# A scan and feed-forward layer on one core: three output tiles of each batch made in two halves

## What is computed

```
zxbcdt = u @ in_proj_w.T                       # 512 -> 2368 columns: z, x, B, C, dt
xBC = silu(causal_conv4(xBC) + conv_b)         # four taps in time, per channel
y = chunked_scan(x, dt, A, B, C) + x * D       # chunks of 64 tokens, 64 heads of 16
yg = y * silu(z)                               # 1024 channels
yn = yg * rsqrt(mean(yg * yg) + eps) * norm_weight
x = layernorm(u + yn @ out_proj_w.T)           # 1024 -> 512 columns: the output tiles
x = layernorm(x + ffn(x))                      # second stage, not touched
```

## Time and profile before

| | us |
|---|---|
| median of 3 runs | 1950.24 |
| lowest and highest | 1948.11, 1953.44 |
| profiled execution | 1956.19 |
| its span, first to last instruction | 1954.3 |
| TensorE matmuls busy | 1720.0 (88%) |
| VectorE busy | 1419.7 (73%) |
| GpSimd busy | 1002.5 (51%) |
| ScalarE busy | 938.2 (48%) |
| mean granted TensorE clock | 0.912 |

### The profile page before, as it was taken

How to read it: one execution, slowest core, us unless ns; L and a number is a source line. 1 busy time by engine, 2 the same in 40 slices (tenths; PEclk the granted TensorE clock), 3 DMA queues, 4 the chain that set the end, 5 groups by cost and what they waited for, 6 DMA issues and landing times.

```text
span 1954.3 us, 37182 instructions
## 1 busy us (share of the span) xinstructions
PE 1720.0 (88%) x11168; PEld 886.9 (45%) x11168; DVE 1419.7 (73%) x2295; ACT 938.2 (48%) x1647; POOL 1002.5 (51%) x1031
## 2 busy tenths in 40 slices
PE   2688889798888888988888897988799999999998
PEld 1244445445444454554454454455344444444443
DVE  6758757858766876686776688597677777777775
ACT  2463253344335426343533533442576666666662
POOL 0045436525444543552554365276577676777774
PEclk9898998898898888888889888987899999999999
DMA  6110140122014013112301401363011111011111
GB/s 208 48 47 26 41 98 19 39 61 73 24 41 110 26 35 79 39 38 49 90 25 41 98 26 41 70 186 54 33 33 55 33 55 45 33 54 54 33 34 54
DMA packets 214679, 109.66 MB, mean 56 GB/s; under 512 B 133796, under 2 KB 185696, under 8 KB 214496
## 3 DMA queue, kind: packets, MB, share of 16 engines
q1 hardware_dynamic: 214496, 107.37, 20.7%
HBM read 80.57 MB, written 26.76 MB: 55 GB/s over the span
## 4 chain that ended last, share of the span: by engine, by line
PE 56%; DVE 25%; issue 9%; SPq 4%; DMA 2%; ACT 2%; DVEq 1%; POOL 0%; ACTq 0%; POOLq 0%
PE ps_in L794 12%; PE ps_in L926 7%; PE ps_in L772 7%; PE ps_yo L941 6%; PE ps_yd L941 6%; PE ps_yo L852 5%; DVE pre L1271 5%; PE ps_s L926 4%; PE ps_t L926 4%; DVE mix L1360 4%; DVE state L1375 2%; PE ps_t L819 1%; SPq L543 1%; DVE res L1428 1%; PE ps_d L830 1%
## 5 line engine op out<-in xcount | busy, mean ns | idle before, releaser
L1077 ACT ACTIVATE decay<-ps_d 128x512 f32<-128x512 f32 x256 | 151.8, 593 | 333.2 <-PE ps_d L830 267.8
L772 PE MATMUL ps_in<-u_hi,w_hi 128*128 128x512 f16 (+1 forms) x608 | 238.0, 391 | 55.7 <-DVE u_lo L1258 34.1
L1360 DVE TENSOR_TENSOR mix<-decay,gb 128x512 f32<-128x512 f32 x256 | 227.1, 892 | 63.0 <-PE ps_yd L842 30.3
L1660 POOL TENSOR_TENSOR xend<-xpad,decay 128x256 f32<-128x256 f32 x256 | 180.7, 726 | 160.0 <-PE ps_yo L865 132.4
L794 PE MATMUL ps_in<-w_out,zg 128*128 128x512 f32 x512 | 253.0, 651 | 6.1 <-DVE pre L1271 6.1
L772 PE MATMUL ps_in<-u_lo,w_hi 128*128 128x512 f16 (+1 forms) x608 | 237.4, 390 | 0.0
L772 PE MATMUL ps_in<-u_hi,w_lo 128*128 128x512 f16 (+1 forms) x608 | 236.7, 389 | 0.0
L1752 POOL TENSOR_TENSOR gate_sum<-gate_sum,gate_part 128x512 f32<-128x512 f32 x88 | 142.2, 1616 | 104.6 <-DVE gate_part L1581 104.2
L1271 DVE SCALAR_TENSOR_TENSOR pre<-ps_in,cws,pre 128x511 f32<-128x511 f32 (+2 forms) x240 | 178.9, 746 | 8.6 <-ACT pre L1016 2.8
L794 PEld LDWEIGHTS ps_in<-w_out,zg 128*128 128x128 f32 x512 | 107.6, 217 | 133.3 <-issue 124.5
L852 PE MATMUL ps_yo<-bc,state 128*128 128x64 f32 x896 | 152.2, 341 | 16.9 <-DVE state L1375 16.8
(11 more groups left out here) (182 smaller groups left out, 3844.3 us busy)
## 6 DMA issues: line engine op xcount, KB each, us to landing
ebc<-e_dram SPq DMA_DIRECT2D x256, 64.0 KB, 2.6
u<-u_t SPq DMA_DIRECT2D x9, 1024.0 KB, 5.2
res<-u_tok SPq DMA_DIRECT2D x32, 256.0 KB, 2.7
x_dram<-res SPq DMA_DIRECT2D x32, 256.0 KB, 2.0
xa<-x_dram SPq DMA_DIRECT2D x8, 1024.0 KB, 5.7
xr<-x_dram SPq DMA_DIRECT2D x32, 256.0 KB, 2.6
out<-xr SPq DMA_DIRECT2D x32, 256.0 KB, 2.0
fw_words<-gu_words SPq DMA_DIRECT2D x32, 176.0 KB, 3.0
```

The source lines that it names most:

```text
L772: last = mm(ps_in[bk][0:m, :], w[:, k, col:col + m], u[:, k, :], start=(k == 0 and j == 0), stop=(k == KT - 1 and j == 2))
L1077: ac(decay[:, n % NG, :, :].rearrange("p a b -> p (a b)"), ps_d[n % 2][:, :], ACT.Exp).then_inc(e_done, 1)
L1360: v.tensor_tensor(mix[:, n % NG, :, :], decay[:, n % NG, :, :], gb[:, c % 2, 0:CH].unsqueeze(1).broadcast_to([P, CT, CH]), ALU.mult).then_ ...
L1660: g_.tensor_tensor(xend[:, pairs, :], xpad[:, c % 2, pairs, :], decay[:, g, :, CH - 1:CH].broadcast_to([P, CT, 2 * HD]), ALU.mult).then_in ...
```

## The change

`out_proj` takes a range of its eight matmuls. The waits stand ahead of the first, the release behind the last. `use_in` on TensorE makes matmuls 4 to 7 of an output tile in the tile's own slot, and matmuls 0 to 3 in the slot before, behind that slot's own uses. For o0, o1 and o2 these are slots 13, 21 and 29. o3, in the tail, goes through `use` and stays whole. No other engine's list changes.

```diff
-            def out_proj(st, tt):
+            def out_proj(st, tt, tiles=range(CT)):
                 bk, free, _ = st.bank(f"o{tt}")
-                pe.wait_ge(gate_done, st.scan * NC + 2 * tt + 2)
-                need(pe, in_free[bk], free)
-                for k in range(CT):
+                if 0 in tiles:
+                    pe.wait_ge(gate_done, st.scan * NC + 2 * tt + 2)
+                    need(pe, in_free[bk], free)
+                for k in tiles:
                     last = mm(ps_in[bk][:, :], zg[:, k, tt * P:(tt + 1) * P], w_out[:, k, :],
                               start=(k == 0), stop=(k == CT - 1))
-                last.then_inc(in_full[bk], 1)
+                if CT - 1 in tiles:
+                    last.then_inc(in_full[bk], 1)
...
             def use_in(st, slot):
                 for name in st.at(slot):
-                    use(st, name)
+                    if name[0] == "o":
+                        out_proj(st, int(name[1]), range(CT // 2, CT))
+                    else:
+                        use(st, name)
+                for name in st.at(slot + 1) if slot + 1 < SLOTS else []:
+                    if name[0] == "o":
+                        out_proj(st, int(name[1]), range(CT // 2))
```

## The result

The changed kernel takes 1987.01 us (median of 4 runs, 1978.71 to 1990.10); the kernel before, on the same chips, 1949.66 us. The ratio is 1.0182, 95% interval 1.0147 to 1.0217: slower by 1.5 to 2.2%, some 37 us. The forecast was 1979.3 us, +29.1.

A forecast was written before the change was run, and what follows sets the result against it. TensorE alone was taken to set the end from `within` to `res`. Seven batches at +34.2 us in all, less 5.1 in the last, gave +29.1; against the median 1950.24 us that is 1979.3, range 1955 to 2004.

The forecast's parts named there:

- The wait for the taps: TensorE's first half waits for VectorE's taps, ending 3.9 us after `within` starts today; total wait about 134 us plus fourth tiles.
- The state's wait: TensorE's 0.62 us wait for the state, ahead of `from_before`, goes because the state is then long ready.
- The full-clock sum: From the old start of `within` to `res` at full clock: 14.24 us for first and second tile, 13.58 for the third.
- The clock comes back 4.0 us after the first pass: TensorE starts the first half at 1.2 GHz after its pause and stays there 4.0 us, losing 2.0 us a tile.
- 3.3 us of new wait: Each split tile pays 3.3 us of new wait on TensorE; the shorter low-clock stretch gives 2 of them back.
- Low stretches about as many, and shorter: In the profile after, TensorE's stretches at 1.2 GHz would be about as many as before, and shorter.
- Per tile +1.48, +1.33, +2.08: Added time from `within` to `res` for first, second, third tile: +4.9 a batch, +34.2 us over seven batches.
- The last batch gains 5.1 us: No projection, so no taps in the way: first tile unchanged, second gains 2.9 us, third 2.2, together -5.1.
- the clock at once: Rival: in the split tiles the clock comes back as soon as today, loss 1.15 us; +11.3 us, 1961.5; chance 0.15.
- the clock low throughout: Rival: the clock stays low through the whole first half, loss 3.44 us a tile; 2014 us; chance 0.08.
- Rival 4: Nothing measurable: VectorE's 4.5 to 6.7 us of waiting for the tile takes up the shift; 1951 us; chance 0.11.
- Rival 3: First half fills the pause ahead of `within` if taps end below some 2.4 us after its old start; 1801; chance 0.04.

The follow-up runs named there:

- the pause filled: The changed kernel with 28 extra matmuls ahead of the wait for the taps in slots 13, 21 and 29, first seven batches: 1947.35 us, ratio 0.9960.
- the fastest one: The changed kernel with VectorE's taps of x0, x3, x6 one slot earlier and 8 extra matmuls ahead of the first half: 1865.54 us, ratio 0.9544.

## Why the prediction was right

Point by point, as the prediction put it:

- *The wait for the taps comes to the surface, 3.9 us after the old start of `within`.* Right in all 21 tiles. The first pass comes 4.17 us after `y_all` at o0, 4.09 at o1 and 4.17 at o2, less 0.14 for `within`'s own start: 4.0 us, and 3.93 were taken. That is 0.07 to 0.15 us after the taps end, as named. The wait for the taps grew from 6.1 to 147.5 us, where 134 plus that of the fourth tiles was named; the third tiles, whose pause was longer before, wait 7.7 us and not 6.4. Moving the half behind `within` (ratio 1.0011) and moving the taps ahead of it (0.9725) both remove the loss, the one cause from two sides.
- *The state's wait goes, and the other engines are covered.* Right: `mixing` and `y_before` start late, by 3.07 and 1.36 us of idle time, and VectorE still waits 2.25 us for the tile.
- *The full-clock sum, 14.24 us from the old start of `within`, 14.38 from `y_all`.* With the pause filled, o0 takes 14.63: the sum is 0.25 us short, of which 0.1 is in the first pass. For o2 13.72 was the sum on that scale, and it took 14.01.
- *The clock comes back 4.0 us after the first pass, a loss of 2.0.* It came back 4.33, 3.83 and 4.12 us after it (between 2.8 and 6.1 in single tiles), 4.1 in the mean. The rows after a pause came nearer than those of the output tiles, which said 2.3. That the mean of four rows met the mean of 21 tiles to 0.1 us is in part luck: single tiles spread by 3 us, and o2 split alone had it back after 3.2 us, o1 split alone after 4.9. The run with the pause filled puts the loss at 1.9 in the mean.
- *3.3 us of new wait, and the shorter low stretch gives 2 of them back.* Right in kind, too large in both: 2.6 to 3.0 us of wait, and 1.0, 1.6 and 0.2 us back by the table above. The two errors have opposite signs, and their difference came out nearly right.
- *Low stretches about as many, and shorter.* Not so in the tiles: they have 9.8, 10.7 and 10.2 us where they had 10.2, 10.2 and 7.8. What is less is the work that falls into them.
- *Per tile +1.48, +1.33, +2.08; 34.2 us for 21.* The tiles gave +1.87, +1.40, +2.41, or 39.7, so this term was 5.5 us too small, mainly by the full-clock sum of o0 and o2 (0.25 and 0.29 us). It stood at 34.75 at the last batch because of things the prediction did not have: in the seven heads of batches the clock was at the low level for 90.6 us before and for 67.1 after, and they are 7.4 us shorter; and the last batch's o0, for which no change was expected, is 1.7 us longer, with waits of 0.40 us for GpSimd and 0.59 for a DMA ahead of its first half. So the size of the total is in part luck, while its sign and the term itself are not.
- *The last batch gains 5.1 us.* It gained 5.2, but divided otherwise: o1 and o2 gained 2.6 (14.36 to 11.78, from the start of `within` before and of the first pass after) and 0.9 (13.02 to 12.08), not 2.9 and 2.2. The `res` of o3 follows that of o2 1.5 us sooner (13.34 us against 14.86), where a low stretch of 3.4 us is gone.
- *Total +29.1.* The profiled executions say +29.7. The medians say +37, interval 29 to 42 us; the changed kernel's four runs spread over 11 us, and the profiled one is the second fastest.

Of the rivals, the clock at once (1961.5) and the clock low throughout (2014) both lie outside the four runs. Rival 4, that nothing can be measured, is excluded by the interval. Rival 3 named its point of decision, where the taps end; the run that moved the taps has shown that it decides.

## What to carry to other kernels

Work that is moved ahead in an in-order list takes its waits with it, and everything it is moved past then waits for them: look up, for each moved step, when its latest wait is met, not whether there is idle time in front. If the wait is late, move what ends it first; the same split that lost 1.8% won 2.7% once the taps stood a slot earlier. And price a pause of TensorE with the clock that follows it: a few cheap matmuls in pauses of 2.4 to 3.7 us were worth 2.3% here, though they compute nothing.

## What was not expected of the hardware

The clock also falls around a short pause, and it can fall when the dense work has already begun. With the taps early, TensorE stood 1.90 us, and the granted clock of the stretch with the pause and of the next one is

```profile
305.00:307.40 2.40, 0.58 (x4) 0.30 (x3) 2.33 (x5) 1.21 (x3) 0.59 (x1) 1.00 0.00 0
307.40:311.30 3.90, 3.82 (x5) 1.65 (x6) 3.76 (x8) 0.00 (x0) 1.58 (x1) 0.57 0.00 0
```

full during the pause and low for most of the first half behind it. This order is the rare one: in two of the 21 tiles the clock fell after the first pass, in the other 19 up to 2.7 us ahead of it, which at o1 is ahead of the pause itself. The pause does not stand alone, either: TensorE had stood 1.25 us ahead of the small matmuls in front of it,

```profile
304.48 0.38 PE L786 MATMUL ps_in<-ones,ssum 128*128 128x1 f32 x2 [1.25 <-DVE pre L1279]
```

and from there to the pause it was at work for 1.1 us (304.48 to 305.58). In these tiles the clock came back 4.6 to 5.9 us after the first pass in the mean of each of the three tiles, later than after the pause of 6.4 us in the changed kernel (4.1): a shorter pause did not bring a shorter low stretch into the dense work.

The five operations of `dt_second` on VectorE (`dtd`) took 3.40 us at this place in the changed kernel and 5.56 in the fastest one, for the same shapes. The first of the five makes most of the difference: 0.42 us in the one, 2.16 in the other, where it ran from 306.89 to 309.05, beside an operation of GpSimd:

```profile
306.39 2.38 POOL L1685 TENSOR_TENSOR state_d<-state,dec 128x1024 f32<-128x1024 f32 x1
```

In the changed kernel that operation was over at 324.22, and the five began at 324.96. Both kernels with early taps and no fill have 5.15 us there too. That the two operations hindered each other is argued from these rows; no run sets them apart.
